# Three gathered columns of six groups fetched by TensorE with one-hot products in the attention passes of a graph network

## What is computed

```python
x_proj = h @ W                       # 4 heads of 16
e = leaky_relu(alpha_s[src] + alpha_d[dst] (+ edge term), 0.2)
m = segment_max(e, dst)
w = exp(e - m[dst])
denom = segment_sum(w, dst)
out = segment_sum(w[..., None] * x_proj[src], dst) / denom
```

## Time and profile before

| | us |
|---|---|
| median of 3 runs | 13213.82 (13212.54 to 13214.28) |
| span of the profiled execution | 13211.9 |
| GpSimd busy | 9802.5 (74%) |
| VectorE busy | 6811.8 (52%) |
| ScalarE busy | 4061.7 (31%) |
| TensorE busy, products / weight loads | 517.1 (4%) / 338.5 (3%) |

### The profile page before, as it was taken

The page is one execution under the profiler, slowest core; times in us unless marked ns, Lnnn a source line. Parts: engine busy times, 40 slices in busy tenths (PEclk is TensorE's granted clock), DMA queues, the critical chain, the costliest instruction groups (busy, mean ns, idle before and its releaser), DMA issues. The chain is left out here.

```text
span 13211.9 us, 103483 instructions
## 1 busy us (share of the span) xinstructions
PE 517.1 (4%) x1768; PEld 338.5 (3%) x1768; DVE 6811.8 (52%) x10645; ACT 4061.7 (31%) x4014; POOL 9802.5 (74%) x10362
## 2 busy tenths in 40 slices
PE   3000001100000200000010000000000000000001
PEld 1000000100000200000000000000000000000000
DVE  2777876377777533333333333343333336656656
ACT  4333333233333311111111111111111113666663
POOL 7777776777777677777777777777777776777775
PEclk9999999555555655555555555555555555555555
DMA  8445444344444222222212222222222223444443
GB/s 334 120 123 129 123 123 107 90 123 123 123 122 124 64 66 65 63 65 66 63 45 61 61 63 62 60 49 58 62 61 61 61 63 89 160 160 156 162 160 116
DMA packets 977609, 1316.81 MB, mean 100 GB/s; under 512 B 660939, under 2 KB 676770, under 8 KB 963551
## 3 DMA queue, kind: packets, MB, share of 16 engines
q10 hardware_dynamic: 558595, 803.76, 18.8%
q0 software_dynamic: 334400, 373.85, 14.8%
q1 hardware_dynamic: 83996, 134.02, 2.8%
HBM read 651.23 MB, written 659.53 MB: 99 GB/s over the span
## 5 line engine op out<-in xcount | busy, mean ns | idle before, releaser
L1862 POOL DMA_INDIRECT c_y<-g_tab,srcs x4545 | 4291.3, 944 | 1386.9 <-issue 1386.9
L2318 POOL DMA_INDIRECT c_y<-h_tab,srcs x1547 | 1461.0, 944 | 506.4 <-issue 471.4
L824 POOL DMA_INDIRECT c_y<-h_tab,srcs x1531 | 1444.9, 944 | 467.1 <-issue 467.1
L824 POOL DMA_INDIRECT first_y<-h_tab,srcs x1452 | 1370.6, 944 | 445.2 <-issue 442.6
L1894 DVE TENSOR_TENSOR c_s<-c_y,c_ad 128x64 f32<-128x64 f32 x300 | 79.6, 265 | 1905.2 <-DMA c_y<-g_tab,srcs 1873.7
L1979 ACT ACTIVATE c_ex<-c_de 128x64 f32<-128x64 f32 x300 | 67.9, 226 | 3171.7 <-issue 2847.4
L1930 DVE COPY c_w_in<-c_ex 128x64 f32<-128x64 f32 x300 | 66.8, 223 | 1580.1 <-ACT c_ex L1979 1580.1
L1938 DVE TENSOR_TENSOR_SCAN c_acc<-c_r,c_w_in 128x1156 f32<-128x1156 f32 x300 | 753.9, 2513 | 10.4
L846 DVE TENSOR_TENSOR_SCAN c_q_all<-c_mask,c_q_in 128x408 f32<-128x408 f32 (+2 forms) x800 | 734.3, 986 | 16.3 <-issue 8.8
L890 DVE TENSOR_TENSOR_SCAN c_acc<-c_r,c_w_in 128x408 f32<-128x408 f32 (+2 forms) x800 | 732.0, 978 | 6.9
L939 ACT ACTIVATE c_q_in<-c_q_raw 128x1552 f32<-128x1552 f32 (+1 forms) x200 | 596.7, 2983 | 271.8 <-DVE c_q_in L906 197.5
(11 more groups left out here) (405 smaller groups left out, 6432.2 us busy)
## 6 DMA issues: line engine op xcount, KB each, us to landing
c_y<-g_tab SPq DMA_DIRECT2D x12288, 0.3 KB
rows_d<-c_row ACTq DMA_DIRECT2D x96, 2048.0 KB, 6.9
rows_d<-c_row ACTq DMA_DIRECT2D x288, 576.0 KB, 2.9
c_q_raw<-q_start ACTq DMA_DIRECT2D x194, 776.0 KB, 6.2
rows_d<-c_row ACTq DMA_DIRECT2D x192, 784.0 KB, 4.3
c_y<-h_tab SPq DMA_DIRECT2D x6144, 0.2 KB
c_y<-g_tab ACTq DMA_DIRECT2D x6144, 0.3 KB
q_start<-first_y SPq DMA_DIRECT2D x97, 776.0 KB, 8.9
```

The costliest lines, as they stand in the source:

```text
L824: nc.gpsimd.indirect_dma_start(y[:, g % NY, k, 0:D], None, h_tab, source(g, k))\
L1862: nc.gpsimd.indirect_dma_start(y[:, g % NY, k, :], None, g_tab, source(g, k))\
L2318: nc.gpsimd.indirect_dma_start(y[:, g % NY, k, :], None, h_tab, source(g, k))\
```

## The change

Columns 14 of slot 2, 15 of slot 3 and 13 of slot 5 are no longer fetched by GpSimd in the 16 rounds of six groups (`MATCHED`, `NMATCH` = 48 columns a pass). For each, the set-up stores the 128 source node numbers as 4-byte floats (`match_d`). ScalarE loads them, spread over all partitions, into `spare`. VectorE compares them with the node numbers of a tile (`ids`, in PSUM bank `pb`), 49 tiles at a time: the result, 128 nodes by 49 x 128 edges of zeros and ones, is half a column's selection. TensorE multiplies each 128 x 128 piece with the tile of `gt` and adds up over 98 tiles in `pa`, 128 edges by 72 columns, and VectorE copies that into the slot. The first half's selection takes the place of `h`, the second has a buffer of its own (`match_b`, which also takes the place of `ad_raw`). Each group has one half: VectorE compares for the half column ahead, TensorE multiplies it.

The cut diff; renamed tiles of the join at a pass's end (`vt`, `mt`, `rt`, `wt` now parts of `spare`), the set-up's list of steps, and the unused `valid` are left out.

```diff
+HC = NC // 2
+MATCHED = [(2, GW - 2), (3, GW - 1), (NY - 1, GW - 3)]
+NMATCH = len(MATCHED) * NACT
...
+                    for m, (slot, k) in enumerate(MATCHED):
+                        lo = NTABLE + m * NACT
+                        sp.dma_start(src_i[lo:lo + NACT, :], by_column[slot * GW + k:NY * GW * NACT:NY * GW, :])\
+                            .then_inc(src_loaded.h, 16)
...
+                sp.dma_start(match_d, src_f[NTABLE:NTABLE + NMATCH, :]).then_inc(places_stored.h, 16)
...
-        ad_raw, ad = st.sb("ad_raw", [P, ET, H]), st.sb("ad", [P, H, ET])
+        match_b, ad = st.sb("match_b", [P, HC * P]), st.sb("ad", [P, H, ET])
+        ad_raw = match_b[:, 0:ET * H].rearrange("p (t h) -> p t h", h=H)
+        match = [t.rearrange("p (c e) -> p c e", e=P) for t in (h[:].rearrange("p c f -> p (c f)"), match_b[:])]
+        spare = st.sb("spare", [P, 4, P])
...
-            ps_e = [st.ps(f"ps_e{b}", [P, 512]) for b in range(2)]
+            e_bank = st.ps("ps_e", [P, 512])
+            ps_e = [e_bank[:, b * H * GW:(b + 1) * H * GW] for b in range(2)]
+        ids = pb[:, 0:NC]
...
-        taken = SYNC_SLOTS + [ACT_SLOT]
+        taken = SYNC_SLOTS + [ACT_SLOT] + [slot for slot, _ in MATCHED]
...
             @block.tensor
             def _(pe):
+                def edge_scores(i, b, pieces=0):
+                    if not isinstance(i, int) or i or b:
+                        pe.wait_ge(*eadded(i * 2 + b + pieces))
...
+                def fetch_half(q, half):
+                    pe.wait_ge(*made(q * 2 + half + 1))
+                    pe.nop(nofuse=True)
+                    if half == 0 and (not isinstance(q, int) or q):
+                        pe.wait_ge(*copied(q))
+                        pe.nop(nofuse=True)
+                    for k in range(HC):
+                        last = nc.tensor.matmul(pa[:, 0:TG], match[half][:, k, :], gt[:, half * HC + k, :],
+                                                start=half + k == 0, stop=half * HC + k == NC - 1)
+                    last.then_inc(mixed.h, 1)
+
+                def group(n, j, fetch=True):
+                    if bd is not None:
+                        edge_scores(n * (NY // 2) + (j + 1) // 2, (j + 1) % 2)
+                    if fetch:
+                        fetch_half(n * 3 + 1 + j // 2, j % 2)
...
             @block.vector
             def _(v):
-                def step(pc, slot, use):
+                def compare(at, half):
+                    v.tensor_tensor(match[half], spare[:, at, :].unsqueeze(1).to_broadcast([P, HC, P]),
+                                    ids[:, half * HC:(half + 1) * HC].unsqueeze(2).to_broadcast([P, HC, P]),
+                                    ALU.is_equal).then_inc(made.h, 1)
+
+                def matches(n, j, more=True):
+                    if j % 2 == 0:
+                        slot, k = MATCHED[j // 2]
+                        v.wait_ge(*mixed(n * 6 + j + 2))
+                        v.tensor_copy(y[:, slot, k, :], pa[:, 0:TG]).then_inc(copied.h, 1)
+                    if more or j < 4:
+                        v.wait_ge(*match_loaded((n * 3 + (1, 3, 5)[j // 2]) * 16))
+                        v.wait_ge(*mixed(n * 6 + j + 1))
+                        compare((1 + j // 2) % 3, j % 2)
+
+                def step(pc, slot, use, *turn):
...
+                    v.wait_ge(*row_ready[b](i))
                     for k in range(H):
...
                     if pc.next_w:
-                        if b == 0:
-                            v.wait_ge(*row_ready[1](i))
-                        else:
-                            v.wait_ge(*row_ready[0](i + 1))
...
+                    if turn:
+                        matches(*turn)
 
                     v.wait_ge(*exps(g + 1))
...
+                v.tensor_copy(ids, node[:, 0:NC]).then_inc(ready.h, 1)
+                v.wait_ge(*ready(3))
+                v.wait_ge(*match_loaded(16 * 3))
+                compare(0, 0)
...
+                compare(0, 1)
...
             @block.scalar
...
-                    send(piece(i, b))
                     if j < NPART:
...
+                    send(piece(i, b))
+                    if more and 1 <= j <= 3:
+                        next_sources(n, j)
```

More of the change, by code:

```diff
@@ L435, in begin @@
         h_turned, hts_ready, q_mixed, q_ready = (st.sem(n, NBLOCK) for n in ("h_turned", "hts_ready", "q_mixed", "q_ready"))
-        vs = st.chain("setup_steps", """node upto valid none_at first1 first deg has hneg none1 none2 start2 starti last
+        vs = st.chain("setup_steps", """node upto none_at first1 first deg has hneg none1 none2 start2 starti last
             lastc lasti cur prev same pen eq cnt cont contpen whole1 whole dst0 row fixf fix_at wide turned
@@ L735, in _ @@
                 act.wait_ge(*firsts_loaded(16))
-                act.wait_ge(*vs.before("valid"))
+                act.wait_ge(*vs.before("none_at"))
                 find(0)
@@ L998, in conv_edges, with softmax_join @@
         st.close()
-    def softmax_join(st, rows, H, J, pa, pb, row_stored):
+    def softmax_join(st, rows, H, J, pa, pb, row_stored, spare=None):
         F = H * (J + 1)
         mrep, got = st.sb("mrep", [P, F]), st.sb("got", [P, F + H])
-        vt, mt = st.sb("vt", [F, P]), st.sb("mt", [F, P])
+        if spare is None:
+            spare = st.sb("spare", [P, 4, P])
+        vt, mt, rt, wt = (spare[0:F, k, :] for k in range(4))
         ms, vs_ = st.sb("ms", [F, P + 1]), st.sb("vs", [F, P + 1])
-        rt, wt = st.sb("rt", [F, P]), st.sb("wt", [F, P])
         vin, min_, mall = st.sb("vin", [P, F]), st.sb("min", [P, F]), st.sb("mall", [P, F])
@@ L1034, in on_scalar @@
         def on_scalar(act):
[L1035 removed]
+            for name, t in (("exp_r", rt), ("exp_w", wt), ("exp_in", e_in[:]), ("exp_row", e_row[:])):
                 act.wait_ge(*ch.before(name))
[L1037 removed]
+                act.activation(t, t, ACT.Exp).then_inc(ch.h, 1)
         def on_vector(v):
@@ L1867, in _ @@
             def _(pe):
-                if bd is not None:
[L1869 to L1877, removed]
+                def edge_scores(i, b, pieces=0):
+                    if not isinstance(i, int) or i or b:
+                        pe.wait_ge(*eadded(i * 2 + b + pieces))
+                        pe.nop(nofuse=True)
+                    pe.wait_ge(*e_loaded[b](i * 16 + 16))
+                    pe.nop(nofuse=True)
+                    nc.tensor.matmul(ps_e[b], ea[:, b, :], bd[:], start=True, stop=True).then_inc(e_scored[b].h, 1)
+                def fetch_half(q, half):
+                    pe.wait_ge(*made(q * 2 + half + 1))
+                    pe.nop(nofuse=True)
+                    if half == 0 and (not isinstance(q, int) or q):
+                        pe.wait_ge(*copied(q))
+                        pe.nop(nofuse=True)
+                    for k in range(HC):
[7 more added lines that the diff above has]
+                        fetch_half(n * 3 + 1 + j // 2, j % 2)
+                if bd is not None:
+                    edge_scores(0, 0)
+                for half in range(2):
+                    fetch_half(0, half)
+                with pe.Fori(0, NACT - 1) as n:
+                    for j in range(NY):
+                        group(n, j)
+                for j in range(NY):
+                    group(NACT - 1, j, j < 4)
+                if bd is not None:
+                    edge_scores(HALF - 1, 1, 1)
                 fix_on_tensor(pe)
@@ L1893, in step @@
                         v.wait_ge(*act_got((use + 1) * (16 * P)))
+                    for m, (matched, _) in enumerate(MATCHED):
+                        if slot == matched:
+                            v.wait_ge(*copied(use * 3 + m + 1))
                     v.tensor_tensor(s0[:, :, 0:w], ys[:, :, D:D + H].rearrange("p t h -> p h t"), ad[:, :, cols],
@@ L2021, in group, with sources, next_sources @@
                         load_places(n + 1)
+                    send(piece(i, b))
+                    if more and 1 <= j <= 3:
+                        next_sources(n, j)
+                def sources(at, n):
+                    act.dma_start(spare[:, at, :], match_d[bass.ds(n + at * NACT, 1), :].to_broadcast([P, P]))\
+                        .then_inc(match_loaded.h, 16)
+                def next_sources(n, j):
+                    act.wait_ge(*made(n * 6 + (0, 4, 2, 6)[j]))
+                    act.wait_ge(*match_loaded((n * 3 + 2 + j) * 16))
+                    sources((0, 1, 0, 2)[j], n + 1)
+                for at_row in range(3):
+                    sources(at_row, 0)
                 load_places(0)
```

63 lines of the change are left out of this document (33 added, 30 removed).

## The result

| | us |
|---|---|
| before, median of 4 runs beside the changed kernel | 13214.05 (13212.54 to 13218.14) |
| after, median of 4 runs | 14757.04 (14755.41 to 14758.62) |
| after over before | 1.1167, 95% interval 1.1151 to 1.1182 |
| span of the profiled execution after | 14753.6 |

The changed kernel is 1543 us slower.

A forecast was written before the change was run, and what follows sets the result against it. GpSimd's row fetches, 1.249 us a column, bound the kernel now; after the change, 47 pairs a pass at 2 x 21.25 + 7.3 = 49.8 us add 555 + 2 x 529 = 1613 to 13213.8: 14,825 us, range 13,025 to 15,440.

The forecast's parts named there:

- the central case: TensorE's clock at its lower level throughout the passes: 14,825 us, own range 14,600 to 15,440, chance 0.57.
- The level of the clock: TensorE's granted clock in the attention passes was claimed to stay at the lower level, 0.50, with records about 0.21 us apart.
- the first rival: TensorE's clock rises inside each half, which takes 11.3 to 14 us; GpSimd stays the bound, 13,035 us; chance 0.33.
- The reason I gave: Low clock because 72 columns move only 0.12 of each 0.213 us, like the set-up's 100 us with exposed weight loads.
- Duration of a half: TensorE's 49 products, 98 records at 0.213 us, plus 0.35 us for first load, last end and signals: 21.25 us.
- Between the halves: VectorE's copy 0.25, comparison 6.75 and gaps 0.3 us lie between two halves on TensorE: 7.3 us.
- The bound of 12.1 us: Upper bound for VectorE's comparison from the strided attention product; as a rival with high clock 13,350 us, chance 0.04.
- A pair of groups: Two groups in an attention pass take two halves of 21.25 us and 7.3 us between them: 49.8 us.
- A pass: First to last score addition: 28 + 47 x 49.8 + 30 = 2399 us against 1870; first pass +555, others +529.
- The point P = 15.1 us: Length of a half, comparison's end to last product, at which two groups reach GpSimd's 37.5 us; shorter halves are hidden.
- What a GpSimd column is worth: Each indirect fetch column on GpSimd costs 1.249 us; 144 fewer save 180 us if GpSimd stays the bound.
- VectorE's wait: VectorE's copy out of `pa` waits some 21 us for TensorE in each pair of groups.

The follow-up runs named there:

- run 1: Changed kernel with each one-hot product reading 128 columns of the node tile in place of 72 (last tile 72): 13033.33 us, 0.9864 of before.
- run 6: Changed kernel with each one-hot product reading 100 columns of the node tile in place of 72 (last one 72): 13061.34 us.
- run 7: Changed kernel with each one-hot product reading 114 columns of the node tile in place of 72 (last one 72): 13060.81 us.
- run 2: Changed kernel multiplying only 34 of the 49 pieces of each half, comparisons kept whole, fetched columns incomplete: 13031.39 us.
- run 5: Changed kernel multiplying only 42 of the 49 pieces of each half, comparisons, copies and waits kept, fetched columns incomplete: 13914.27 us.

## Why the prediction was right

The forecast was 14,825 us, the time 14757.04. The range, 13,025 to 15,440, held gains and losses alike, so that the time lies in it says little; what was tested is the central case and the steps below it.

- **The level of the clock.** 0.50 through all halves, as forecast. This step carried everything: with the clock risen the same edit gives 13,033 (run 1), where the first rival said 13,035, and its half, put at 11.3 to 14 us, took 11.06 to 14.12. The 11.3 is an estimate, 98 records 0.11 us apart by the starts of the earlier trace rows and 0.4 us; at a granted clock of 1.00 whole halves took 11.13 (below). The chance of 0.33 it had was not too much. The reason I gave holds only in part. That the width of the moving operand matters is borne out: with 72 columns the clock stayed at 0.50 although TensorE was busy throughout, with 128, 100 and 114 it rose to 0.98, 0.99 and 1.00 (runs 1, 6, 7). That 72 columns take 0.12 us of a record is an estimate, half of the 0.24 between the 144-column records of the earlier trace rows; no run shows it. But the other half of the reason, taken from the weight loads of the set-up, is not borne out: run 1 has a load for each record (46 and 46 in 7720 to 7725) and the clock rises. That the set-up's 100 us without a pause ran at the low level is the author's estimate from its 529-ns records, against a clock column of 1.00; no row shows a load that TensorE waited for there, and why the records took 529 ns was not tried. Since these rows were what tipped the choice to the lower level, part of this step was luck.
- **Duration of a half.** 98 records at 0.213 us: measured 20.95 us from one half's start to the next, 0.2138 a record. Right. That 72 columns would take 0.213 was an estimate, since the earlier trace rows have no record of this width; the changed kernel showed 0.2138 with 72 and run 1 0.214 with 128. The 0.35 us for the first load, the last product's end and the signals was an estimate too, which no run shows by itself. I added it to each half; it is paid once a pair, since the second half follows the first without a gap: 42.06 us for two in place of 42.5. This is the term that was mis-sized.
- **Between the halves.** 7.3 us forecast, 7.29 measured; the comparison 6.69 where 3136 elements and 1.06 ns for each further one gave 6.8, taken as 6.75. The bound of 12.1 us from the strided product was far off: with one input in PSUM and one row spread over 49 tiles the comparison took 1.07 ns for an element, no more than the 1.10 of the widest contiguous instruction.
- **A pair of groups.** 49.8 forecast, 49.35 measured. 47 pairs in each of three passes at 0.45 us less are 63 us; the forecast was 68 too high.
- **A pass.** 2399 forecast for the later ones, 2368.4 measured; 21 us of the difference are the pairs. I had the second comparison behind the first score addition; it lies ahead of it (4717.76, then the addition at 4724.35), so some 7 us moved from inside each pass to before it and changed no sum. Behind the last copy come 28.0 us (12417.4 to 12445.4) where I had 30. The 7 us more that I gave the first pass for its start also lie ahead of its first score addition, in the 14.4 us there. In the first pass a pair takes 49.75 us (4753.09 to 4802.84), 0.40 more than later, and the pass 20.3 us more (2388.7 less 2368.4); 20 were forecast for the edge products.
- **What hides and what doesn't.** The point P = 15.1 us held: 14.75 us (run 2) is hidden, 18.13 (run 5) costs 863 us less than 21.1, and the line from there down meets GpSimd's bound at about 15.0. What a GpSimd column is worth held too: 178.5 us for 144 columns (180 forecast).
- **VectorE's wait** for the copy: 2962.3 us over 144 copies, 20.6 each, where 49.8 less twice 14.4 gave 21.
- **Small slips of the working.** 1515 columns over 98 groups are 15.5 and not 15.4, and 14,825 + 3 x 202 is 15,431 and not 15,440. Nothing else hangs on them.

## What to carry to other kernels

An operation that is moved to an idle engine has to be priced per turn of the loop that it now closes, here two halves and the comparison between them, and against the old bound's turn: the idle share of the engine says nothing on it. Where products move few columns for each weight load, look at the granted clock in 5-us stretches within a burst and not only at the busy share, and try wider moving operands, even with columns that nobody uses. Take from the bound engine only as much as the slower path can carry: two columns of six groups gained 122 us where three lost 1543.

## What the runs showed of the hardware

- A stream of 4-byte products, each with its own 128 x 128 weights and 72 moving columns, kept TensorE busy in 20.00 of 20 us (7700 to 7720, changed kernel) and its granted clock at 0.50 through whole halves of 21 us; with 100, 114 or 128 columns and no other difference it stood at 0.93 to 1.00 in the 5 us after the first 4 to 5 us of the halves shown (0.99 and 1.00 from 7740 in runs 6 and 7; 0.98 from 7720 and 0.93 from 7740 in run 1).
- At the lower clock such a record costs 0.214 us with 72 as with 128 columns, so the wider product was free. The weight loads too were busy in 20.00 of the 20 us from 7700 (changed kernel), 333 ns each at the median; that the load of 128 weights sets the record would fit this, but no run changed the load. At a granted clock of 1.00 it is 0.11 us with 100 and with 128 columns (11.13 / 98, rows below).
- After the pause of 6 to 8 us between halves the clock was back at 0.50 for the first microseconds (run 1, 7715 to 7720), and rose anew. Not every half began low: where the pause was 0.78 us (100 columns) or 2.99 us (128), the granted clock was 1.00 in the whole half:

```profile
7715.36 11.13 PE L1904 MATMUL c_pa<-gt,c_match_b 128*128 128x100 f32 x98 [0.78 <-DVE c_match_b L1932]
7772.83 11.13 PE L1904 MATMUL c_pa<-gt,c_match_b 128*128 128x128 f32 x98 [2.99 <-DVE c_match_b L1932]
```

These are halves of run 6 and of run 1, 98 records in 11.13 us each. What decides when the clock rises was not tried and stays open.
- A comparison over 128 x 6272 elements with one input in PSUM takes 6.69 us, 1.07 ns an element, where an elementwise instruction over 3136 took 1.10.
